# Index columns and the written-out GpSimd program in a graph network's convolution edge stages

## The reference

```python
e0 = f0[edge_src]
e1 = f1[edge_src]
...
mid0 = w0 * e0 * sh0
mid1 = w3 * jnp.einsum('eum,em->eu', e1, sh1) / jnp.sqrt(3.0)
mid2 = w1[:, :, None] * e0[:, :, None] * sh1[:, None, :]
mid3 = w2[:, :, None] * e1 * sh0[:, :, None]
...
    s = jax.ops.segment_sum(v, edge_dst, num_segments=n)
    return s / cnt.reshape((n,) + (1,) * (v.ndim - 1))
n0, n1 = (smean(mid0), smean(mid1))
n2, n3 = (smean(mid2), smean(mid3))
```

## Time and profile before

| | |
|---|---|
| median of 3 runs | 5688.06 us (5687.17 to 5689.68) |
| profiled execution, its time | 5691.12 us |
| its span, first to last instruction | 5689.3 us |
| TensorE busy | 4587.4 us (81%) |
| VectorE busy | 4072.7 us (72%) |
| GpSimd busy | 3297.1 us (58%) |
| ScalarE busy | 2192.9 us (39%) |
| mean granted TensorE clock | 0.817 of 2.4 GHz |

### The profile page before, as it was taken

One profiled execution on the slowest core, in us unless ns is written; L12 is line 12 of the kernel. 1 busy time (PEld: TensorE's weight loads), 2 busy tenths in 40 slices (PEclk: granted clock), 3 DMA queues, 4 the chain that ended last, 5 costly groups with the idle time before them and its releaser, 6 DMA issues. The chain is left out here.

```text
span 5689.3 us, 73586 instructions
## 1 busy us (share of the span) xinstructions
PE 4587.4 (81%) x14104; PEld 2009.0 (35%) x14104; DVE 4072.7 (72%) x10653; ACT 2192.9 (39%) x5204; POOL 3297.1 (58%) x3685
## 2 busy tenths in 40 slices
PE   0699987776999999999999900888879788887665
PEld 0233335552333333333333200333347533334554
DVE  1466659996887888787788787444459855556999
ACT  0223325553222222222222256333349833334555
POOL 0366669995344434443443244666657666667998
PEclk9999988787777777777777755898989899898877
DMA  9222227662222222122212199222249722225665
GB/s 363 81 67 67 68 56 226 215 216 71 52 56 52 53 52 56 51 54 51 56 50 50 28 344 339 62 66 66 66 136 356 275 63 69 66 67 152 196 192 162
DMA packets 545392, 678.01 MB, mean 119 GB/s; under 512 B 57166, under 2 KB 387106, under 8 KB 545052
## 3 DMA queue, kind: packets, MB, share of 16 engines
q1 hardware_dynamic: 451888, 496.01, 28.4%
q0 software_dynamic: 86400, 142.71, 9.1%
q10 hardware_dynamic: 7020, 38.40, 1.6%
HBM read 449.48 MB, written 245.49 MB: 122 GB/s over the span
## 5 line engine op out<-in xcount | busy, mean ns | idle before, releaser
L500 POOL DMA_INDIRECT aggregates<-agg_out,scatter_index x600 | 616.3, 1027 | 413.4 <-issue 253.3
L1231 ACT ACTIVATE y_chunk<-residual,ln_minus_mean_rstd,ln_rstd 128x160 f32<-128x160 f32 x1568 | 703.3, 555 | 377.3 <-POOL ln_minus_mean_rstd L1294 289.8
L755 POOL TENSOR_TENSOR edge_ln_rstd<-edge_ln_var,minus_half 128x16 f32<-128x16 f32 x50 | 146.9, 2938 | 854.6 <-DVE edge_ln_var L1011 854.6
L1197 PE MATMUL psum<-self_weights,x_chunk_T 128*128 128x160 f32 (+1 forms) x2352 | 491.9, 362 | 61.5 <-DVE node_mid L1322 29.3
L576 PE MATMUL psum<-identity,scaled_x 128*128 128x128 f32 x600 | 146.5, 282 | 486.0 <-DVE scaled_x L650 315.6
L1290 POOL TENSOR_TENSOR ln_rstd<-ln_var_eps,minus_half 128x4 f32<-128x4 f32 x392 | 441.0, 1125 | 145.3 <-DVE ln_var_eps L1379 85.7
L859 PE MATMUL psum<-rbf_times_sh,weights_layer 64*96 64x512 f32 (+1 forms) x600 | 513.7, 1040 | 2.4 <-DVE leaky_and_tanh L1016 1.6
L483 POOL DMA_INDIRECT gathered<-x_layer,gather_index x400 | 397.3, 993 | 176.2 <-issue 120.1
L1197 PEld LDWEIGHTS psum<-self_weights,x_chunk_T 128*128 128x128 f32 x2352 | 413.9, 224 | 108.1 <-issue 63.6
L1387 DVE BATCH_NORM_STATS2 ln_stats<-residual 128x6 f32<-128x160 f32 x1568 | 389.5, 308 | 0.1
L483 POOL DMA_INDIRECT gathered<-in_x,gather_index x200 | 207.5, 1038 | 229.3 <-DVE scaled_x L650 142.0
(11 more groups left out here) (202 smaller groups left out, 11059.7 us busy)
## 6 DMA issues: line engine op xcount, KB each, us to landing
x_layer<-y_chunk SPq DMA_DIRECT2D x294, 320.0 KB, 5.1
x_chunk<-x_layer SPq DMA_DIRECT2D x294, 320.0 KB, 4.7
agg_chunk<-aggregates SPq DMA_DIRECT2D x196, 320.0 KB, 5.5
sh_rows<-in_sh_big SPq DMA_DIRECT2D x50, 768.0 KB, 5.8
agg_chunk<-aggregates SPq DMA_DIRECT2D x98, 384.0 KB, 5.9
aggregates<-agg_out ACTq DMA_DIRECT2D x48, 768.0 KB
x_chunk<-in_x SPq DMA_DIRECT2D x98, 322.0 KB, 3.0
agg_chunk<-aggregates SPq DMA_DIRECT2D x98, 322.0 KB, 3.7
```

Of the source, the lines that this page charges most:

```text
L500: eng.indirect_dma_start(agg_table[:, :], bass.IndirectOffsetOnAxis(idx_last[:, q, b:b + 1], 0), agg_out[:, q, b, :], None, bounds_check=N ...
L1197: eng.matmul(o[:, b, 0:ns + 96], x_t[:, k4, (2 * half + b) * 128:(2 * half + b) * 128 + 128], self_w[:, k, 0:ns + 96], start=b == 0, stop= ...
L1231: op = eng.activation(y_out[:, buf, b, :], res[:, buf, b, :], ACT.Identity, bias=shift[:, buf, b:b + 1], scale=rstd[:, buf, b:b + 1])
```

## The change

In the convolution edge stages, GpSimd's program no longer uses `steps`: a Python loop writes out all 53 steps, so `s` is a plain number in each. The index columns are taken from `src_i` and `last_i` directly, one column for each DMA. The two copies, their semaphores, the waits for them and the waits that protected the copied buffers are gone. The other engines' programs and the attention layer are as before.

```diff
--- before.py
+++ after.py
@@ -239,7 +239,7 @@
                           "rows_in1 scaled scaled1 attr_2 self_in self_ready self_zeroed small_in table_zeroed weights_in zeroed")
 
         conv_sems = sems("edge", "agg aprod aprod_v attr0 attr1 back e_mm fact gather0 gather1 hidden hidden_mm "
-                                 "index index_used products proj scan_s scan_v scatter0 scatter1 transposed vec_m "
+                                 "products proj scan_s scan_v scatter0 scatter1 transposed vec_m "
                                  "vec_y w_copied w_mm xa xq xs_act xt_copied ya")
         EDGE = {0: conv_sems, 2: conv_sems, 3: conv_sems}
         EDGE[1] = sems("edge1", "a_less_max agg aggr applied applied_v av_mm beta av_read back carried carry decay den "
@@ -465,42 +465,27 @@
             if l == 0:
                 eng.wait_ge(P["last"], 1)
 
-            def step(s, par):
-                held(eng, N - 1)
+            for s in range(NG + 3):
+                par = s % 2
                 if live(s, 0, NG):
-                    g = s
-                    read = held(eng, (g - par) * 32, S["gather0"])
-                    now, before = held(eng, g + 1, S["index"]), held(eng, g - 1, S["xs_act"])
-                    apart(eng)
-                    wait(eng, S["gather1"] if par else S["gather0"], read)
-                    eng.tensor_copy(idx_src[:, par, :], src_i[:, bass.ds(g * T, T)]).then_inc(S["index"], 1)
-                    apart(eng)
-                    wait(eng, S["xs_act"], before)
-                    wait(eng, S["xq"], before)
-                    wait(eng, S["xa"], before)
-                    eng.wait_ge(S["index"], at(S["index"], now))
+                    wait(eng, S["xs_act"], s - 1)
+                    wait(eng, S["xq"], s - 1)
+                    wait(eng, S["xa"], s - 1)
                     for b in range(T):
+                        col = s * T + b
                         eng.indirect_dma_start(gathered[:, par, b, 0:width], None, x_table[l][:, :],
-                                               bass.IndirectOffsetOnAxis(idx_src[:, par, b:b + 1], 0))\
+                                               bass.IndirectOffsetOnAxis(src_i[:, col:col + 1], 0))\
                            .then_inc(S["gather1"] if par else S["gather0"], 16)
                 if live(s, 3, NG):
-                    g = s - 3
-                    q = 1 - par
-                    sem = S["scatter1"] if q else S["scatter0"]
-                    if isinstance(g, int) and g == 0 and l == 0:
+                    g, q = s - 3, 1 - par
+                    if g == 0 and l == 0:
                         eng.wait_ge(P["table_zeroed"], table_zeroed)
-                    read, now = held(eng, (g - q) * 32, sem), held(eng, g + 1, S["agg"])
-                    apart(eng)
-                    wait(eng, sem, read)
-                    eng.tensor_copy(idx_last[:, q, :], last_i[:, bass.ds(g * T, T)]).then_inc(S["index_used"], 1)
-                    apart(eng)
-                    eng.wait_ge(S["index_used"], at(S["index_used"], now))
-                    eng.wait_ge(S["agg"], at(S["agg"], now))
+                    wait(eng, S["agg"], g + 1)
                     for b in range(T):
-                        eng.indirect_dma_start(agg_table[:, :], bass.IndirectOffsetOnAxis(idx_last[:, q, b:b + 1], 0),
+                        col = g * T + b
+                        eng.indirect_dma_start(agg_table[:, :], bass.IndirectOffsetOnAxis(last_i[:, col:col + 1], 0),
                                                agg_out[:, q, b, :], None, bounds_check=N - 1, oob_is_err=False)\
-                           .then_inc(sem, 16)
-            steps(eng, NG, step)
+                           .then_inc(S["scatter1"] if q else S["scatter0"], 16)
 
         def edge_scalar(eng, l):
             S = EDGE[l]
```

## The result

The changed kernel took 5740.93 us (median of 4 runs, 5736.23 to 5777.76), the kernel before 5688.41 (5687.17 to 5689.68): a ratio of 1.0107, 95% interval 1.0075 to 1.0139. Forecast were 5510 us and a range up to 5565, so the prediction was wrong, and by its sign. The profiled execution took 5736.23 us with a span of 5734.4.

The account below looks back on a forecast made before the run. GpSimd, working or issuing 98% of the step, was taken to bound the kernel. Savings of 1.48 + 1.50 + 0.92 = 3.90 us a step, times 46 = 179, plus 2, minus 3, gave 178: 5688.06 to 5510, range 5465 to 5565.

Parts of the forecast that it names:

- Part 1: GpSimd's edge steps: without both copies and the long gaps behind them, its own step becomes 11.03 us, 1.53 less.
- The collision: Stretching of GpSimd's work by VectorE's scan: expected to move from the gather copy to the first gather, 0.36 us a step.
- Part 2: GpSimd's edge program: dropped landing waits, register operations and loop branch gain nothing; the moved waits cost nothing.
- Part 3: Two-step loop through gathers, agg_out and scatters limits next: 10.98 us a step in layer 2, 11.73 in layer 0.
- The clock: TensorE's granted clock in layers 2 and 3: 0.94 or more, with about half the clock loss going.
- Kept clock losses: Rival: TensorE falls to 1.2 GHz as often as before; 139 us saved, about 5549 us; chance 0.20.
- GpSimd alone: Rival: only GpSimd binds, so every edge step gains the full 1.53 us; 5475 us; chance 0.10.
- The straight-line program not fed in time: Rival: GpSimd's written-out code is fetched too slowly, gaps of 0.65 cost about 145 us, 5833 us; chance 0.05.
- from ScalarE's first read to its finished agg_out: Layer 2's term in the two-step loop for work from gathered rows to agg_out: 8.53 us, read from 3880.42 to 3888.95.
- the signs that I had named against myself: Gaps of 1 to 3 us between DMAs at regular distances, clock staying at 0.90, or landing time beyond 1.8 us.
- the landing: Time for gathered rows to land, a term of layer 2's two-step loop: 1.76 us.

Follow-up runs that it names:

- the one edited kernel with a pause that met the hold-up: Changed kernel plus an unread copy, waited for, ahead of each step's scatters, run on chip 11: 5686.68 us, ratio 0.9983 to the kernel before.
- the control: The changed kernel unedited, measured again on chip 8 against the kernel before: 5541.56 us, ratio 0.9738.

## Why the prediction was wrong, and where it was right

**Where nothing is held up, its steps can be read one by one.** Windows of the kernel after on chip 5, same 46 steps:

```profile
219.05:765.76 546.71, 521.03 (x1655) 199.14 (x1654) 371.22 (x737) 179.73 (x415) 381.50 (x368) 0.99 0.27 73
3541.04:4080.82 539.78, 498.18 (x1566) 212.23 (x1565) 290.72 (x412) 231.06 (x504) 380.35 (x368) 0.94 0.26 73
4465.58:4992.52 526.94, 485.88 (x1566) 201.00 (x1565) 295.68 (x412) 216.72 (x550) 381.15 (x369) 0.95 0.27 74
```

A step takes 11.89, 11.73 and 11.46 us; forecast were 11.9, 11.3 and 11.2. Together these stretches take 1613.4 us, on record 1814.8: the difference of 201.4 covers all that lies between the two spans, 5535.1 and 5734.4.

*Part 1, GpSimd's step of 11.03.* A little too high. Its timeline on chip 5, with the VectorE scan that one gather meets:

```profile
3898.22 0.99 POOL L476 DMA_INDIRECT gathered<-x_layer,src_index  x1 [0.30 <-issue]
3899.18 1.28 DVE L652 TENSOR_TENSOR_SCAN running_vectors<-segment_goes_on,running_vectors,vector_message 96x512 f32<-96x512 f32 x1
3899.52 1.72 POOL L476 DMA_INDIRECT gathered<-x_layer,src_index  x1 [0.30 <-issue]
3901.55 0.95 POOL L476 DMA_INDIRECT gathered<-x_layer,src_index  x1 [0.30 <-issue]
3904.06 1.02 POOL L486 DMA_INDIRECT aggregates<-agg_out,last_index  x1 [0.30 <-issue]
3909.26 0.99 POOL L476 DMA_INDIRECT gathered<-x_layer,src_index  x1 [0.30 <-issue]
```

From first gather to first gather 11.04 us, every gap 0.30 in this step. The collision didn't vanish; it moved, but to the second gather (1.72 us, to 3901.24), not to the first. What stretches it is the scan L652: in the three windows 81 gathers took more than 1.2 us, and every one of them began during this scan and ended 0.78 to 0.81 us after it (here 3900.46 and 3901.24). The other scan, L645, which reads one input from PSUM, stretched none to 1.2 us. GpSimd by line, layer 2:

```profile
L476 POOL DMA_INDIRECT gathered<-x_layer,src_index x184 | 195.7, 1063 | 56.1 <-issue 54.2 <-ACT agg_out L539 1.8
L486 POOL DMA_INDIRECT aggregates<-agg_out,last_index x184 | 184.7, 1004 | 117.4 <-issue 59.6 <-ACT agg_out L539 57.4 <-DVE scaled_x L635 0.3
```

Busy time and issue gaps are (195.7 + 184.7 + 54.2 + 59.6) / 46 = 10.74 a step, 0.29 under the forecast. The DMAs take 8.27 where I had 8.14 and 0.36 for the collision, and the gaps 2.47 where I had 2.53.

The Trainium skill (SBUF — State Buffer, "Who interferes with whom") infers for VectorE's two-input `tensor_tensor` that it leaves descriptor generation alone. Here the scan, which also reads two inputs from SBUF, stretches the gathers, whose issuing reads the index column from SBUF too.

*Part 2, waits at no cost.* Right: the two runs with both copies unread, in which the landing waits are gone, stand within 0.1% of the kernel before.

*Part 3, the two-step loop.* Layer 0 right (11.89 for 11.9, and the least gain). In layers 2 and 3 a term is mis-sized: by the sum, GpSimd waits for agg_out 0.27 and 0.17 us a step over its own 11.03. It waits 0.99 and 0.73 (step less busy time and issue gaps, which are 10.74 and 10.73). The step of its own that I had 0.3 too long hides part of this, which is luck; 0.43 and 0.26 a step are left. That is 46 x 0.69 = 32 us, and 5510 lies 26 to 32 us under the 5535 and 5542. The clock did what was forecast: 0.94 or more.

*The rivals, where nothing is held up.* Kept clock losses (5549): no, the clock rose, though this number lies nearer to the 5542 than mine. GpSimd alone (5475): no, it waits for agg_out in each layer. The straight-line program not fed in time (5833): no; written out alone it costs nothing (ratio 1.0007). The Trainium skill (Runtime: NRT & Kernel Launch, "Instruction fetch mechanics") has the fetching of straight-line code mostly hidden, and this case agrees: 77 instruction packets in place of 59, and no time lost to them.

**The step that failed on record** is the one under *Part 3* that carried the work between gathered rows and finished agg_out over unchanged ("from ScalarE's first read to its finished agg_out", 8.53 us). TensorE hands over at six of its lines in it (L562, L566, L578, L585, L588, L597), each taken at the duration that the profile of before gave. With GpSimd's pauses gone that no longer holds in the measurement on record: one hand-over alone was 8.7 us late, and in that step the 8.53 became 16.90 (3904.84 to 3921.74). The 111 late starts are 311 us in 138 steps, more than the 201.4 us that the stretches lost, so some of it must have fallen where nothing waited. The kernel after then takes 13.74, 12.99 and 12.72 us a step, the clock falls to 0.91 in layer 0 and stays at 0.90 and 0.91 in the others, and GpSimd's lighter step has nothing to work on. That the same kernel loses 200 us in one measurement and none in another was in none of my rivals. Of the signs that I had named against myself, one came (the clock at 0.90), as a consequence. The gaps were 0.30 as forecast in either case, but for three to eight longer ones in each stretch, and the landing took 1.77 us (3903.07 to 3904.84), as before. The gather stretched to 1.3 us and more on average is, on chip 5, the second of a step, not the first.

**Shown and not shown.** Shown: the same kernel gives 5741 and 5765 us in two groups, with the late hand-overs, and 5542 and 5535 in two, without; the one edited kernel with a pause that met the hold-up has shorter delays; the kernel before has none in its trace, and is within 0.3% in all seven groups. Only argued: that the queue of indirect DMAs has to run dry before the news gets through; a third of the late results got through while GpSimd was issuing. Open: what holds the news back at all; whether it belongs to a chip, to the session on it or to the recording, as no numbered chip was met in both ways; and whether bytes or number count. A hold-up with the gathers and scatters left out was not tried.

## What to carry to other kernels

Where an engine waits for the end of its own small copy, it is the wait that costs, not the copy. Where nothing is held up, both copies with their waits make the three stretches 147 us longer (1760.4 on chip 6 against 1613.4 on chip 5, 1.07 us a step), and the scatter copy without the wait costs nothing that can be told (5547 against 5542). A pause of one engine may protect others, so after such a change look for waits that the profile can't match to a releaser, and for a trace with fewer semaphore records than others. And measure the changed kernel itself again on a second chip before you explain a loss. Of what was measured, the version with the waited-for scatter copy is the safer one (0.9842 and 0.9983), the plain one the faster where nothing is held up (0.9729 and 0.9738, against 1.0107 and 1.0113).

## What the hardware showed that was not expected

TensorE's results reached other engines up to 9.8 us late in some measurements and on time in others, with the same instructions. In the other direction, the fastest kernel of all, that with a copy in every fourth step (5495.69 us), owes its lead over the control (5541.56) to a stage that none of these edits touches. Its edge stages are those of the control (1618.9 us against 1614.0), but after them it needs 493 us where the others need 541 to 548. GpSimd's power and a VectorE instruction in this last node stage, there:

```profile
L1280 POOL TENSOR_TENSOR ln_rstd<-ln_var_eps,minus_half 128x4 f32<-128x4 f32 x98 | 100.4, 1025 | 0.5 <-DVE ln_var_eps L1369 0.4
...
L1357 DVE TENSOR_SCALAR angle_whole_turns<-angle_turns 128x8 f32<-128x8 f32 x98 | 14.2, 145 | 0.1
```

and in the control of its chip:

```profile
L1275 POOL TENSOR_TENSOR ln_rstd<-ln_var_eps,minus_half 128x4 f32<-128x4 f32 x98 | 143.6, 1465 | 0.5 <-DVE ln_var_eps L1364 0.4
...
L1352 DVE TENSOR_SCALAR angle_whole_turns<-angle_turns 128x8 f32<-128x8 f32 x98 | 100.6, 1027 | 0.1
```

So both instructions are slower in the usual pattern (1465 and 1027 ns) than in the other (1025 and 145 ns). In a node chunk of the control the VectorE instruction starts during a product of GpSimd and ends with it (5303.81 and 5303.78); in the fast one it starts after that product has ended (5284.01 after 5283.78). All other nineteen traces have the usual pattern. The four executions of that kernel took 5491 to 5507 us, so the other three probably had the better pattern too; what sets it was not settled. It is worth 0.9%.
